# Masked cross-attention layer on one core: the attention stage from float32r and bfloat16 parts to float16 hi/lo pairs under power-of-two scales found on the chip

## What is computed

```python
q = (x @ Wq + bq)      # as (b, 16, 512, 32)
k = (ctx @ Wk + bk);  v = (ctx @ Wv + bv)
scores = einsum('bhqd,bhkd->bhqk', q, k) / sqrt(32)
scores = where(j < i, scores, -1e30)        # key j, query i
attn = softmax(scores);  attn[:, :, 0, :] = 0
h = layer_norm(x + (attn @ v) @ Wo + bo)
out = layer_norm(h + relu(h @ W1 + b1) @ W2 + b2)      # W1: 512 x 2048
```

## Time and profile before

| | |
|---|---|
| device time, median of 3 runs | 2659.24 us (2656.49 to 2664.09) |
| span of the profiled execution | 2657.7 us; its own time is not listed apart from the runs, and its span lies within their range |
| mean granted TensorE clock | 0.991 |
| busy: TensorE, VectorE, ScalarE, GpSimd | 98%, 79%, 58%, 60% |
| instructions | 62,252 |
| SyncE's DMA queue | 266.74 MB, 40.3% of 16 engines' span |

### The profile page before, as it was taken

One profiled execution on the slowest core, in us unless ns is written; L12 is line 12 of the kernel. 1 busy time (PEld: TensorE's weight loads), 2 busy tenths in 40 slices (PEclk: granted clock), 3 DMA queues, 4 the chain that ended last, 5 costly groups with the idle time before them and its releaser, 6 DMA issues.

```text
span 2657.7 us, 62252 instructions
## 1 busy us (share of the span) xinstructions
PE 2605.2 (98%) x22600; PEld 2245.5 (84%) x22600; DVE 2088.3 (79%) x5171; ACT 1530.3 (58%) x2945; POOL 1587.9 (60%) x1721
## 2 busy tenths in 40 slices
PE   7999999999999999988999999999999999999998
PEld 5888888888888888867888888888888888888887
DVE  6888988888888888888767766676767676767675
ACT  4777877787777777766343434343434344444433
POOL 3777777766666666666555555454555555555543
PEclk9999999999999999989999999999999999999999
DMA  6566655565556555656131323222222222222220
GB/s 189 154 154 163 157 152 155 145 166 143 143 145 152 144 142 138 147 140 171 48 67 47 70 50 69 52 66 55 59 62 56 64 57 64 57 65 57 64 55 27
DMA packets 439556, 273.35 MB, mean 103 GB/s; under 512 B 299648, under 2 KB 334400, under 8 KB 439248
## 3 DMA queue, kind: packets, MB, share of 16 engines
q1 hardware_dynamic: 437648, 266.74, 40.3%
q10 hardware_dynamic: 1600, 2.62, 0.5%
HBM read 109.86 MB, written 57.67 MB: 63 GB/s over the span
## 4 chain that ended last, share of the span: by engine, by line
PE 87%; DVE 4%; SPq 2%; issue 2%; POOL 2%; DMA 2%; ACT 1%; ACTq 0%; DVEq 0%; POOLq 0%
PE h_ps L1443 23%; PE acc L1459 20%; PE lin_ps L724 12%; PE lin_ps L720 6%; PE front L1429 6%; PE max_ps L699 6%; PE st_ps L746 6%; PE o_ps L766 4%; PE o_ps L768 3%; PE st_ps L781 2%; POOL prob_lo L435 1%; SPq L866 1%; SPq L360 1%; DVE W L1400 1%; DMA x_in<-in_x 0%
## 5 line engine op out<-in xcount | busy, mean ns | idle before, releaser
L435 POOL TENSOR_TENSOR prob_lo<-probs,prob_hi 128x512 f16<-128x512 f32 (+1 forms) x768 | 785.1, 1035 | 369.2 <-ACT prob_hi L516 365.1
L1443 PE MATMUL h_ps<-x_halves,W 128*128 128x256 f16 x6144 | 757.2, 273 | 3.1 <-ACT hf L1234 1.7
L1443 PEld LDWEIGHTS h_ps<-x_halves,W 128*128 128x128 f16 x6144 | 596.9, 98 | 89.6 <-issue 12.0
L1459 PE MATMUL acc<-W,hs 128*128 128x256 f16 x5376 | 669.6, 273 | 0.0
L1234 ACT ACTIVATE hf<-h_ps,b1s,scale_evac 128x256 f32<-128x256 f32 x512 | 284.7, 562 | 530.5 <-PE h_ps L1443 530.1
L678 DVE CUSTOM_DVE_ANT_0 max_ps<-max_ps,mask_q 128x128 f32<-128x128 f32 (+3 forms) x1024 | 486.2, 506 | 123.6 <-PE max_ps L699 107.6
L1459 PEld LDWEIGHTS acc<-W,hs 128*128 128x128 f16 x5376 | 526.0, 98 | 60.8
L514 ACT ACTIVATE probs<-st_ps 128x512 f32<-128x512 f32 (+1 forms) x768 | 406.4, 529 | 240.5 <-PE st_ps L781 221.2
L1158 POOL TENSOR_TENSOR hf<-hf 128x256 f32<-128x256 f32 x256 | 248.5, 971 | 462.1 <-ACT hf L1234 462.0
L1396 DVE TENSOR_TENSOR hs<-hf,hs 128x896 f16<-128x896 f32 x256 | 286.9, 1141 | 157.4 <-ACT hs L1223 157.3
L516 ACT ACTIVATE prob_hi<-st_ps 128x512 f16<-128x512 f32 (+1 forms) x768 | 406.7, 530 | 0.0
(11 more groups left out here) (121 smaller groups left out, 3797.4 us busy)
## 6 DMA issues: line engine op xcount, KB each, us to landing
heads<-stage SPq DMA_DIRECT2D x748, 128.0 KB, 2.6
raw<-in_xT SPq DMA_DIRECT2D x64, 256.0 KB, 3.0
o_in<-ctx_rows SPq DMA_DIRECT2D x256, 64.0 KB, 2.6
x_in<-in_x SPq DMA_DIRECT2D x32, 512.0 KB, 4.1
x_rows<-x SPq DMA_DIRECT2D x64, 256.0 KB, 2.0
o_in<-x_rows SPq DMA_DIRECT2D x256, 64.0 KB, 2.4
out<-y SPq DMA_DIRECT2D x32, 512.0 KB, 3.1
raw<-in_cT SPq DMA_DIRECT2D x60, 256.0 KB, 3.5
```

What stands on the lines that cost most here:

```text
L435: pool.tensor_tensor(prob_lo[:, k % 4, 0:w], probs[:, k % PROBS, 0:w], prob_hi[:, k % 4, 0:w], ALU.subtract).then_inc(pl_done, 1)
L1443: last = pe.matmul(h_ps[:, f % 2, 0:T], W1[:, aw, j, f * P:(f + 1) * P], x1_halves[:, item.parity, aa, j, :], start=(j == 0 and m == 0), s ...
L1459: last = pe.matmul(acc_products[:, n, :], hs[:, p % HS, aa, n, :], W2[:, p, aw, n, :], start=(p == 0 and m == 0 and n % 2 == 0), stop=(p = ...
```

## The change

1. **Float16 pairs.** `acts` (the split activations), the three weights, `stage`, `heads` and the maxima's rows become float16, high part and remainder. V has two parts, not three.
2. **Scales.** Each raw chunk is multiplied by a power of two before it is split, and the bias, the exponential's scale and the last multiplication take it back. For each sequence VectorE finds the largest absolute value of ctx and of x by partition (`LOOK`, four reductions over 1,024 elements each), joins them (`TOPS`), SyncE sends them to DRAM (`SPREAD`) and back to all partitions (`GATHER`), and VectorE turns the maximum into powers of two (`RANGE`, six small operations). For the first sequence, the weights and the biases the same is done ahead of everything else (`first_look`, `first_join`, `first_ranges`), once for v, ctx, k and once for x, q.
3. **Places.** `LIN` moves from 32 to 40, and all that hangs on it with it; FEED_AFTER from 30 to 38. x and ctx have four raw chunks each of their own, the scan has its own, the activations are double-buffered by the sequence's parity. The feed stage's memory is laid out anew, so that some of its waits for attention go and others come.
4. The masks of the maximum scores stay in VectorE's one operation, and the mask matmuls of the transposed scores stay.

The diff, cut to its core:

```diff
-    VW = 3 * HD + 2
+    VW = 2 * HD + 2
-    CTX_LOAD = 14
-    CTX_SPLIT = 24
-    X_LOAD = 27
-    X_SPLIT = 33
-    LIN = 32
+    LOAD = {"c": 0, "x": 8}
+    LOOK = {"c": 5, "x": 13}
+    TOPS = 16
+    SPREAD = 17
+    GATHER = 20
+    RANGE = 24
+    SPLIT = {"c": 28, "x": 40}
+    SPLIT_STEP = 3
+    LIN = 40
...
-        acts = {"c": sb("ctxT", [P, 2, KT, S], F32R), "x": sb("xT", [P, 2, KT, S], F32R)}
-        stage = sb("stage", [P, 2, 2, 2, S], F32R)
-        W = {w: sb(f"w{w}", [P, 2, KT, D], F32R) for w in "vkq"}
-        raw = sb("raw", [P, RAW, D], F32)
-        V = sb("V", [P, 2, QT, HEADS, VW], BF16)
-        heads = sb("heads", [P, GROUPS, 2, 4, S], F32R)
+        acts = sb("acts", [P, 2, 2, 2, KT, S], F16)
+        raw = {"c": sb("raw_c", [P, KT, S], F32), "x": sb("raw_x", [P, KT, S], F32)}
+        W = {w: sb(f"w{w}", [P, 2, KT, D], F16) for w in WEIGHTS}
+        stage = sb("stage", [P, 2, 2, 2, S], F16)
+        scan = sb("scan", [P, KT, D], F32)
+        heads_at = sb("heads", [P, GROUPS, 2, 4, S], F16)
+        V = sb("V", [P, 2, QT, HEADS, VW], F16)
...
     def sync(sp):
-                for j in range(KT):
-                    for item, _ in after_first(due(window, s, SLOTS, B, X_LOAD + 2 * j)):
-                        wait_for(sp, lo_done, NCHUNK, item, chunk_of("c", j) + 1)
-                        sp.dma_start(raw[:, j, :], src).then_inc(raw_loaded[j], 16)
+                for kind in KINDS:
+                    for j in range(KT):
+                        for item, _ in after_first(due(window, s, SLOTS, B, LOAD[kind] + j)):
+                            wait_for(sp, lo_done, NCHUNK, item, chunk_of(kind, j) + 1 - NCHUNK)
+                            load(kind, item, j)
...
+                for item, _ in after_first(due(window, s, SLOTS, B, SPREAD)):
+                    wait_for(sp, top_ready, 1, item, 0)
+                    sp.dma_start(top_rows, top[:, :]).then_inc(top_spread, 16)
+                for item, _ in after_first(due(window, s, SLOTS, B, GATHER)):
+                    wait_for(sp, top_spread, 16, item, 0)
+                    sp.dma_start(gathered[:, 0:P, :].rearrange("p r k -> p (r k)"),
...
     def vector(dve):
         def split(item, kind, j):
-            dve.tensor_tensor(acts[kind][:, 1, j, :], raw[:, j, :], acts[kind][:, 0, j, :], ALU.subtract
+            dve.scalar_tensor_tensor(out=act_part(item, kind, 1)[:, j, :], in0=raw[kind][:, j, :],
+                                     scalar=inverse[:, item.n % 3, i:i + 1], in1=act_part(item, kind, 0)[:, j, :],
+                                     op0=ALU.mult, op1=ALU.subtract).then_inc(lo_done, 1)
...
-        first_split(FIRST_TURN, split_first)
+        for half in range(2):
+            first_look(0, 3, half, first_loaded["v"][2 * half:2 * half + 2], first[:, 0, :, :])
+            first_look(0, 0, half, raw_loaded["c"][2 * half:2 * half + 2], raw["c"])
...
+        first_ranges(0)
+        first_join(1, 5)
+        for w, j in FIRST_TURN:
...
+        first_ranges(1)
...
+                for kind in KINDS:
+                    for half in range(2):
+                        for item, _ in after_first(due(window, s, SLOTS, B, LOOK[kind] + 2 * half)):
+                            for j in (2 * half, 2 * half + 1):
+                                wait_for(dve, raw_loaded[kind][j], 16, item, 16)
+                            dve.tensor_reduce(top_parts[:, KINDS.index(kind), half:half + 1],
+                                              raw[kind][:, 2 * half:2 * half + 2, :].rearrange("p i n -> p (i n)"),
+                                              AX_X, ALU.max, apply_absolute_value=True).then_inc(top_seen, 1)
...
-                                          o[:, :, 0:3 * HD].rearrange("p q (c d) -> p q d c", c=3),
+                                          o[:, :, 0:2 * HD].rearrange("p q (c d) -> p q d c", c=2),
...
-                        for item, _ in due(window, s, SLOTS, B, OUT + 4 * n + 2):
-                            wait_for(dve, v_mid, QT, item, t + 1)
-                            dve.tensor_tensor(V[:, item.parity, t, :, 0:HD], vr,
-                                              V[:, item.parity, t, :, 2 * HD:3 * HD], ALU.subtract
-                                              ).then_inc(v_lo, 1)
...
     def tensor(pe):
-                        pe.matmul(o[:, 0:3 * HD + 1], prob_hi[:, k % 4, col:col + P], v[:, 0:3 * HD + 1],
+                        pe.matmul(o[:, 0:2 * HD + 1], prob_hi[:, k % 4, col:col + P], v[:, 0:2 * HD + 1],
-                        last = pe.matmul(o[:, HD:3 * HD + 1], prob_lo[:, k % 4, col:col + P],
+                        last = pe.matmul(o[:, HD:2 * HD + 1], prob_lo[:, k % 4, col:col + P],
```

More of the change, by code:

```diff
@@ L123, in __init__ @@
         self.small_loaded = sem("scan_small_loaded")
+        self.small_seen = sem("scan_small_seen")
+        self.loaded = [sem(f"scan_loaded{n}") for n in range(2)]
         self.seen = sem("scan_seen")
@@ new lines, in first_look, with first_bias @@
+        def first_look(i, column, half, loaded, tile):
+            for one in loaded:
+                dve.wait_ge(one, 16)
+            dve.tensor_reduce(first_part[:, i, column, half:half + 1],
+                              tile[:, 2 * half:2 * half + 2, :].rearrange("p i n -> p (i n)"), AX_X, ALU.max,
+                              apply_absolute_value=True).then_inc(first_seen[i], 1)
+        def first_bias(i):
+            dve.wait_ge(const_loaded, 32)
+            dve.tensor_reduce(first_part[:, i, 2, 0:1], bias[:, i, :], AX_X, ALU.max,
+                              apply_absolute_value=True).then_inc(first_seen[i], 1)
@@ L570, in vector @@
             for s in range(SLOTS):
-                if window == 0:
-                    first_split(FIRST_SPLITS.get(s, []), split_first)
+                if window == 0 and s in FIRST_SPLITS:
+                    for j in range(KT):
+                        split_weight(FIRST_SPLITS[s], j)
+                if (window, s) == (0, FIRST_X_SPLIT):
+                    for j in range(KT):
+                        split(Item(0), "x", j)
                 if (window, s) == (0, SLOTS - 1):
@@ L719, in linear @@
                         if kind == "v":
[L720 removed]
+                            last = pe.matmul(lin_ps[:, n % 2, :], act_part(item, side, aw)[:, j, t * P:(t + 1) * P],
                                              W[kind][:, aa, j, :], start=(j == 0 and m == 0),
```

520 lines of the change are left out of this document (334 added, 186 removed).

## The result

The changed kernel takes 2828.06 us (median of 4 runs, 2823.75 to 2829.23) against 2658.74 for the one before: 1.0632 times as long, 95% interval 1.0617 to 1.0648. The forecast was 2637, so the time is 191 us over it, 150 over the top of the stated range (2678), and on the other side of no change.

The account below looks back on a forecast made before the run. TensorE was taken to bound the kernel at 70.6 us a sequence, VectorE becoming slower at 68.3: 15 × −2.3 = −34.5, end of attention −4 and −3, start +19, sum −22.5, so 2637 us, range 2585 to 2678.

Parts of the forecast that it names:

- TensorE's sum: TensorE's matmuls after the change: linear 31.1, scores and masks 22.5, values 9.3, together 62.9 us a sequence.
- The upper bound: Top of the range for TensorE's work per sequence, given as 66.3 us; the lower bound was 59.2.
- the wait for x: VectorE's look at x waits for chunks loaded behind head group 0's twelve moves: 4.0 us idle a sequence.
- The rival "the x loads land in time": In attention, no wait at the look; VectorE's 63.3 plus 1.5 decides, 64.8 us a sequence: 2584 us, chance 0.22.
- The start: Before the first splits, maxima go to DRAM and back; VectorE enters the slots at 31, not 10.95: +19 us.
- The fourteen small steps: At the start, mostly dependent range operations after the wide maximum, at 0.2 us each, before the eight splits.
- VectorE's busy time: VectorE's work per sequence after the change, with looks and range steps added: 64.6 us by busy time.
- The 1.3 taken off for overlaps: VectorE's back-to-back operations overlap, some twenty gaps a sequence closing: 1.3 us less, leaving 63.3 us of work.
- 63.3 + 4.0 = 67.3 [...] 0.3 for imperfect overlap: Attention's sequence: VectorE's work plus its idle time, averaging 68.0 with stores, plus 0.3: 68.3 us.
- The end of attention: Last sequence's 24 slots without loads or looks, −4 us, and the mixed stretch around 1200 us, −3.
- ScalarE and GpSimd "have room": In attention, ScalarE (158 us busy of 200) loses four operations, GpSimd (149) is unchanged; neither was to limit.
- The rival on the slower side: In attention, contention with GpSimd lengthens VectorE's operations, 72.4 us a sequence with the idle: 2698 us, chance 0.22.

Follow-up runs that it names:

- run without looks: Changed kernel with constant exponential scale, x chunks and scan tile loaded four slots earlier, and sequences 1 to 15 reusing sequence 0's scales: 2627.29 us, 0.9891.
- float16 kernel without scales: Kernel before with float16 pairs in place of float32r, no scales, no looks, V still in three parts: 2607.83 us, 0.9814 of the kernel before.
- scan late: On looks spread: join and spread one slot earlier, and the scan look eight slots later (slot 10, not 2): 2657.37 us, 0.9999 of the kernel before.
- scan tile earlier: Changed kernel with the W1/W2 scan tile loaded in slot 38 instead of 42, ahead of head group 3's moves: 2798.47 us, 1.0533.
- range steps later: On all three: only the range steps moved, from VectorE's slot 24 to 26, looks left in place: 2697.19 us, 1.0146.
- looks spread: On all three: the four looks moved to slots 6, 9, 11, 14 and the range steps from 24 to 26: 2669.51 us, 1.0049.
- constant scale: Changed kernel with the exponentials' scale an immediate constant instead of a per-partition operand: 2810.21 us, 1.0577.
- the two runs behind: On looks spread, join and spread one slot earlier: 2664.72 us; on that, the scan look eight slots later: 2657.37 us.
- slot numbers alone moved: The whole changed kernel with slot numbers as in scan late and the exponentials' scale operand kept: 2671.25 us, 1.0049.
- all three: Changed kernel with constant exponential scale, x chunks loaded four slots earlier and scan tile loaded four slots earlier: 2729.83 us, 1.0272.

## Why the prediction was wrong

**Right: TensorE's sum.** 62.9 us a sequence forecast, 62.9 in the run without looks. In rows of it without waits (that run, 600 to 1000 us) linear matmuls of 512 columns start 0.215 to 0.217 apart (0.216 forecast), and a value pair takes 0.029 + 0.026 = 0.055 (0.058). Six pairs go from 899.94 to 900.27 us:

```profile
899.94 0.19 PE L968 MATMUL o_ps<-V,prob_hi 128*128 128x65 f16 x1
899.97 0.18 PE L970 MATMUL o_ps<-V,prob_lo 128*128 128x33 f16 x1
...
900.27 0.22 PE L983 MATMUL st_ps<-mask_k,identb 128*128 128x128 bf16 x1
```

The Trainium skill (TensorE: Matmul & The Clock Gate, "Wait — 56ns, not 53.3ns?") has a floor of about 25 ns between starts. The estimate by it, 0.055, was the better value: the next start stands 26 ns behind that of the 33 columns. With 0.055 a pair some 23.0 us of the 62.9 are left for scores and masks, where 22.5 stood: two small errors cancel, so the last digit is luck. The upper bound was added up wrongly: 31.1 + 25.3 + 9.6 is 66.0, not 66.3. The forecast's 1,875 matmuls in 200 us were 1,546 and 1,675, and VectorE was busy 78 to 85%, not 92 or more: the work was right, its share of the time was not.

**Right in kind, near in size: the wait for x.** VectorE was to idle 4.0 us a sequence and 5.4 in the first eight. It idles 2.4 to 3.9 before the look in the later sequences and 6.4 to 7.6 in seven of the first eight. TensorE's pair at slot 16 takes 6.91 us in sequences 8 to 13 and 10.51 in the first eight, in place of 2.7: 4.2 and 7.8. Loading x earlier gave back 52 us, where the sum had 15 × 4.7, some 70. The rival "the x loads land in time" gave 2584 for that; it gave 2776.

**Nearly right: the start.** +19 forecast, bounds 15 and 24. The first matmul stands at 26.65 us (22 to 26 forecast), the first mask matmul 23 later than before; with x loaded earlier, in that run and all built on it, it is 15 to 19 later, so the surplus belongs to the wait for x. Against the float16 kernel without scales (47.5 us) it is 34 later in the changed kernel. VectorE enters the slots at 34.7 (31 forecast). The fourteen small steps took 1.8 us where 2.8 stood; the way over DRAM was slower: from the end of the join at 13.6 to the wide maximum at 21.07 it took 7.4 us where 5.5 stood, and that maximum 1.05 where 0.65 did:

```profile
21.07 1.05 DVE L625 TENSOR_REDUCE first_range<-first_rows_in 128x4 f32<-128x512 f32 x1 [1.86 <-DMA first_rows_in<-first_out]
```

**Small: VectorE's busy time.** 64.6 us a sequence forecast; 195.06 of 200 at 67.6 in scan late, so 65.9:

```profile
800.00:1000.00 200.00, 187.58 (x1896) 109.33 (x1895) 195.06 (x658) 159.86 (x344) 148.05 (x143) 1.00 0.39 105
```

The splits take 1.0 to 1.25 (0.98 forecast), the sum of the outputs 0.418 (0.42). The 1.3 taken off for overlaps rested on "four x subtracts of 0.68 take 2.48"; that row is of the four subtracts of Wq, and the x subtracts of the start don't stand in a row. The form and the size are the same.

**The step that failed** is the line "63.3 + 4.0 = 67.3 [...] 0.3 for imperfect overlap". It takes the sequence as the fullest engine's mean plus its one wait and puts all other waits at 0.3 us. A sequence took 74.7 to 84.9 us, and in scan late, without the wait for x, 67.6 and more, where 63.6 would be left of the line. The line would hold if every engine could run far ahead. Here TensorE can be two units of maximum scores ahead, so where VectorE's slots hold more work than TensorE's for longer than that, TensorE stops, and VectorE's light slots give only part of it back. That is read from the program's waits and the pairs of slots; what the runs price is the list below. I had VectorE's list of slots 9 to 15 in hand for the wait for x and did not make it for the other 41. What it cost, by the runs:

| forecast at | what | shown by | us |
|---|---|---|---|
| 0 | scan tile behind head group 3's moves: `LIN` moved by 8, `SCAN_LOAD` stayed | scan tile earlier | 30 |
| 0 | range steps two slots too early: the wait for the gather, a full stretch, longer operations beside GpSimd | range steps later | 33 |
| 0.3 a sequence | looks stand beside full slots of VectorE | looks spread, less the line above | 28 |
| 0 | exponentials 0.10 us longer by their scale operand | constant scale | 18 |
| 0 | late head moves, scan look in a full slot | the two runs behind | 5 + 7 |

These are 121 us. The rest is in the base: a sequence without the wait for x was forecast at 63.3 + 0.3 = 63.6. In scan late, with no wait for x and a constant scale, late sequences take 67.6: 60 us over 15 sequences. VectorE is busy 65.9 of these, so 2.6 is work over the 63.3 (1.3 in longer operations, and the 1.3 that I took off for overlaps, which busy time kept), and 1.7 is idle. The first seven distances are 71.5 there, 27 us more in all; putting the scan look ahead of GpSimd's mixing gave back 4, and what holds the rest, beside the traffic of the scan and of W2 that only they have, stays open. The end of attention gave nothing of its −7: the last sequence takes 89.7 us from its first mask matmul to its last (90.9 before), and from there to the end it is 1450.3 (1449.1). The start there is 17 and not 19. These are 92 (60 + 27 + 7 − 2); the wait for x, 52 where the sum had some 70, takes 18 off. That comes to 195 and not 191; the parts were measured on different kernels.

**ScalarE and GpSimd "have room".** By share they had, 158 and 149 us of 200. But both stand in a chain between transposed scores and value matmuls, and the exponentials' duration is in it: 18 us in the changed kernel, 14 with slot numbers alone moved. A form of instruction that gets an operand is an added cost like any other; I costed that for VectorE's three-operand forms (+1.4) and never for ScalarE's.

**The rival on the slower side** put 2698 on GpSimd's contention with VectorE. The subtracts did rise, to 1.0 to 1.25 of its 1.38, and a tiny range step took 0.67 us on average where a like operation takes 0.15 at the start:

```profile
23.00 0.15 DVE L647 TENSOR_SCALAR power<-tops 128x1 uint32<-128x1 uint32 x1
```

Counted from the traces (sequences 9 to 13), VectorE is busy 66.1 us a sequence in the changed kernel and 68.8 in all three, where 64.6 was forecast; the rival had 4.4 more than the forecast. So its cause is real, a third of its size in the changed kernel and nearly all of it in all three. But 1.5 us a sequence don't make 191, and the rival's price of 2698 was for this cause and the wait for x together: it named the right side for the smaller part of the causes.

**What the scales cost in the end.** Float16 with two parts of V, by itself, is worth 90 us (2656.6 to 2566.5). The scales, with the looks, places, memory layout and start that come with them, took that back and 171 more. With slot numbers alone moved, the whole change is at 2671; so 157 of these 262 us went by moving steps, with no work left out.

## What to carry to other kernels

When a pipeline's engines are coupled by two buffers, add the work up slot by slot on each engine, and look for stretches in which one engine's work stands over the other's for longer than the buffers cover; the maximum of the two sums is too low. The sum of the maxima of single slots is too high: from the traces (VectorE's busy time in a slot, or TensorE's 1.31 us where that is more; sequences 9 to 13) it is 78.7 us in all three, 74.9 in looks spread and 74.3 in scan late, which take 75.1, 69.0 and 67.6. When a change moves the stages of a pipeline by some slots, list every step whose number stayed (here a load and a look), and read in each queue what it now stands behind. Put added work into slots where its engine has little, and the reader of a round trip over DRAM behind its landing: here the two were 60 us together.

## What the runs showed of the hardware

- ScalarE's activation with its scale from a tile takes 0.10 us longer: 604 to 704 ns for 512 columns, 392 to 485 for 256.
- A stall of TensorE costs more than its length. The table by stage around the look above:

```profile
860.00:869.00 9.00, 9.00 (x100) 5.34 (x99) 6.07 (x19) 8.20 (x16) 5.94 (x6) 1.00 0.39 93
869.50:873.30 3.80, 0.04 (x1) 0.00 (x0) 1.97 (x4) 0.99 (x2) 2.22 (x2) 0.74 0.49 167
873.40:877.40 4.00, 4.00 (x27) 2.42 (x28) 3.76 (x22) 1.20 (x3) 0.47 (x1) 0.50 0.04 7
```

After 3.8 us in which it was busy 0.04, TensorE is granted 0.50, the 1.2 GHz level, over 4 us, and three linear matmuls are listed with 1.49 us where they have 0.81 at 2.4 GHz. From 200 to 1000 us the granted clock is 0.91 to 0.95 in the changed kernel, 0.97 to 0.98 in all three, and 0.97 to 1.00 in looks spread. The forecast priced a wait by its length alone.
- A tiny operation of VectorE that starts beside one of GpSimd can be held until that ends. At 805 us of the changed kernel:

```profile
805.48 1.89 POOL L493 TENSOR_TENSOR prob_lo<-probs,prob_hi 128x512 f16<-128x512 f32 x2
...
805.90 0.75 DVE L681 TENSOR_SCALAR power<-tops 128x2 uint32<-128x2 uint32 x1
...
806.77 0.61 DVE L685 SCALAR_TENSOR_TENSOR exp_scale<-power,exp_unit 128x1 f32<-128x1 f32 x1
```

The last one ends at 807.38, GpSimd's second subtract at 807.37. In four traces (the changed kernel, all three, looks spread, scan late; 100 to 1100 us) I took the six smallest kinds of operations, L681, L685, L779, L817, L819 and L839. All 318 that took over 0.26 us had started while GpSimd was executing and ended 12 to 35 ns after its instruction; none that started without it took as long. So these operations are not fixed at 0.15 to 0.2 us: their time depends on what GpSimd does when they start, and with it on their slot.
